# Attention with a shared expert: q and k split once and stacked through DRAM, output normalised transposed, one large burst every second step

## The chip, the cores and the metric

The kernel runs on one core of a Trainium2 chip. The metric is the device time of one execution in microseconds (us); lower is better.

## The reference

Eight batches of 512 rows with 256 columns are normalised row by row (`xn`). The output is `x + attention(xn) + ffn(xn)`:

```python
def holo_linear(x, basis, phase, amp):            # rank 32
    resonance = jnp.einsum('bli,hi->blh', x, basis)
    return jnp.einsum('blh,oh->blo', resonance, amp * jnp.cos(phase))
q, k, v = (split_heads(holo_linear(x, ...)) for each of q, k, v)   # 16 heads of 16
attn = softmax(jnp.einsum('bhqd,bhkd->bhqk', q, k) * 16 ** -0.5)
out = holo_linear(merge_heads(jnp.einsum('bhqk,bhkd->bhqd', attn, v)), basis_o, phase_o, amp_o)

# ffn: 8 experts of width 352, the best 2 of each row, plus a shared expert of width 704
y = einsum('te,etd->td', combine, expert_out)
return y + (silu(x @ sw_gate) * (x @ sw_up)) @ sw_down
```

All is float32. A matrix product is made exact enough by splitting each operand into a high part (rounded to the format float32r, which TensorE multiplies fast) and a low part (what the rounding left), and adding three products: high by high, low by high, high by low.

## The kernel before

There are three stages. An early one normalises the rows, transposes and splits them (`xn_T_split` in DRAM) and finds the experts of each row. A second one runs 72 tiles of gathered rows through the experts and stores them (`expert_rows`). The late stage, from about 423 us to the end, is the one that the change rebuilds. It does attention and the shared expert for the 8 batches.

The late stage is a software pipeline written out by hand. Each engine runs the same loop `slots`: for each batch b four slots g = 0 to 3, one for each group of four heads, with three slots ahead and two behind; and in each slot eight steps t (`STEPS`). In a step TensorE (PE) does, in this order of its queue:

- `score_T`: the transposed scores of two heads of group g into the pair of banks `st_pair` (two matmuls, 512 columns each). ScalarE (ACT) makes the exponentials of them (`exponent`, `prob`). There is one such pair of banks, so `score_T` of a step waits for `exponent` of the step before.
- `score`: the scores of two heads of the next group into `s_pair`, three steps ahead (`AHEAD`). VectorE (DVE) takes their row maxima (`maximum`, `top`). There is one such pair too, so `score` waits for the `maximum` before it.
- at t = 5 `turn_max`: the maxima, split by `split_max` at t = 4, are transposed; ACT copies them (`max_rows`), and SyncE (SP) puts them by DMA into two extra rows of `q_rows`, so that `score_T` subtracts the maximum. `score_T` of the next slot's t = 0 waits for this.
- at even t `values`: the product of `prob` with the values and a column of ones, which gives the sum of the exponentials with it, into `ot_bank`.
- the rest: small products and the "bursts" of the shared expert.

The rest stands thus in the kernel before. In every slot, at t = 0 to 3, `project` makes q and k of the group after next, for two pairs of heads each, in `m_bank`. The weight `wq_rows` holds each head's columns three times, so that the product comes out as three stacked copies; ACT copies it rounded (`qk_high`) and DVE forms, with a factor of 0 or -1 for each partition (`q_minus`, `k_minus`), the high or low part for each copy (`qk_split`). Four projections in each slot are one chain: each waits for the `qk_split` before, since `m_bank` is one bank. The three ranks-32 products (`low_rank`, n = q, k, v) stand at g = 1, t = 4 and 6, and g = 2, t = 4. The shared expert (`gate_up_shared`: six matmuls of 512 columns) has six tiles f of its width, each a gate and an up; they stand at g = 1 and 3 in every step t = 1 to 6. The sixth tile has only 64 of 128 rows. `tanh` (ACT), `gate_shared`, `hidden_shared` (DVE), `hidden_high` (ACT) and `hidden_low` (GpSimd, POOL) follow. `down_shared` (18 matmuls of 256 columns) stands at g = 2, odd t. The output of batch b-1 is done in g = 0 of batch b: for each 128 rows `turn_o` transposes `o_T`, DVE takes the reciprocal of the 16 sums of each row and multiplies (`normalise`), `turn_back` transposes again, ACT and DVE split; then `low_rank_o` (t = 6) and `project_o` (t = 7) into two banks, which `add_o` adds.

All four compute queues are in order. A wait in one holds all that stands behind it. DMAs are issued by SP, in order too, but for the gathers of `expert_rows`, which POOL issues.

## Time and profile before

| | |
|---|---|
| median of 3 runs | 1241.31 us (1239.57 to 1248.31) |
| the profiled execution | 1241.18 us, of which its span is 1239.4 us |
| busy: PE, DVE, ACT, POOL | 1055.1, 767.2, 601.5, 339.2 us |
| mean granted clock of TensorE | 0.899 of full speed |
| DMA | 73.43 MB, mean 59 GB/s |

The span is the stretch from the first to the last instruction that the profile holds; the 1.8 us around it stay as they are in all sums. "Granted clock" is the share of full speed that TensorE was given. A line of a group gives its busy time, the mean of one instruction in ns and the idle time of its engine before it. Matmuls overlap, so what one costs its queue is read from the starts of two that follow one another, not from its duration.

### The profile page before, as it was taken

How to read it: one execution, taken by the hardware profiler on the slowest of the kernel's cores; microseconds unless marked ns; L12 is line 12 of the kernel's file. 1: busy time of each engine (PE TensorE's matmuls, PEld its weight loads, DVE VectorE, ACT ScalarE, POOL GpSimd, SP SyncE). 2: the span in 40 equal slices, each digit the busy share in tenths (PEclk: the TensorE clock that was granted, in tenths of full speed). 3: DMA queues.
4: the chain of work that ended last, by engine and by line, in shares of the span. 5: the costliest groups of instructions: out<-in, count | busy, mean ns of one | idle time of the engine just before them, and what ended most of it. 6: DMA issues, size and time to landing. Idle time of an engine off the chain costs nothing.

```text
span 1239.4 us, 18708 instructions
## 1 busy us (share of the span) xinstructions
PE 1055.1 (85%) x6090; PEld 698.1 (56%) x6091; DVE 767.2 (62%) x1264; ACT 601.5 (49%) x945; POOL 339.2 (27%) x292
## 2 busy tenths in 40 slices
PE   1750699999999768998998998998998999999986
PEld 1740699999999633554454454454454454454442
DVE  6679533443443356677767767767767767767732
ACT  0231244444444425555655655555555656556652
POOL 1045332222222216106205205304303313312410
PEclk8555599999999967898998998999999999999995
DMA  7664052222222002002102102102102101100100
GB/s 218 237 240 140 17 173 73 68 68 74 69 68 74 33 1 87 1 1 69 35 2 69 36 2 69 36 2 69 36 2 69 35 2 61 44 2 18 53 2 17
DMA packets 47888, 73.43 MB, mean 59 GB/s; under 512 B 7304, under 2 KB 40656, under 8 KB 45776
## 3 DMA queue, kind: packets, MB, share of 16 engines
q1 hardware_dynamic: 41296, 54.74, 12.9%
q0 software_dynamic: 6528, 17.83, 5.1%
q8 instruction: 40, 0.66, 0.2%
q14 instruction: 24, 0.20, 0.1%
HBM read 45.82 MB, written 26.21 MB: 58 GB/s over the span
## 4 chain that ended last, share of the span: by engine, by line
PE 67%; DVE 15%; issue 8%; ACT 5%; DMA 2%; POOL 1%; another core or an unknown queue 1%; SPq 1%; DVEq 0%; ACTq 0%
PE bank L939 10%; PE bank L961 8%; PE st_pair L950 6%; PE bank L841 6%; PE bank L1002 6%; PE s_pair L823 5%; PE st_pair L823 5%; PE s_pair L903 4%; PE bank L892 4%; PE bank L976 3%; ACT prob L682 2%; DVE q_rows L1343 2%; PE bank L831 2%; ACT qk_hi L647 2%; DVE top L1351 2%
## 5 line engine op out<-in xcount | busy, mean ns | idle before, releaser
L1351 DVE TENSOR_REDUCE top<-s_pair 128x2 f32<-128x1024 f32 x256 | 313.3, 1224 | 163.7 <-PE s_pair L903 159.8
L682 ACT ACTIVATE prob<-st_pair 128x1024 f32<-128x1024 f32 x256 | 261.5, 1022 | 217.8 <-PE st_pair L950 214.1
L534 POOL TENSOR_TENSOR h_T<-h_f,h_T 128x512 fp32r<-128x512 f32 (+1 forms) x48 | 61.7, 1286 | 495.9 <-ACT h_T L665 495.9
L950 PE MATMUL st_pair<-q_rows,k_rows 50*128 50x512 f32 x512 | 144.0, 509 | 29.3 <-ACT prob L682 28.6
L950 PEld LDWEIGHTS st_pair<-q_rows,k_rows 50*128 50x128 f32 x512 | 55.8, 189 | 179.9 <-issue 117.6
L939 PE MATMUL bank<-xT_b,w_sh 128*128 128x512 f32 (+1 forms) x576 | 153.8, 402 | 0.0
L961 PE MATMUL bank<-prob,v_ones 128*32 128x512 f32 x1024 | 149.3, 658 | 1.1 <-ACT prob L682 1.1
L903 PE MATMUL s_pair<-k_rows,q_rows 48*128 48x512 f32 x512 | 122.2, 433 | 9.8 <-DVE top L1351 5.5
L510 POOL DMA_INDIRECT xg<-xn_rows,token_of x72 | 68.5, 951 | 210.8 <-PE bank L806 178.5
L939 PEld LDWEIGHTS bank<-xT_b,w_sh 128*128 128x128 f32 (+1 forms) x576 | 101.4, 181 | 32.1 <-issue 6.3
L841 PE MATMUL bank<-w_exp,c_hT 128*128 (+1 forms) x648 | 95.4, 292 | 1.0 <-ACT c_y L617 1.0
L823 PE MATMUL s_pair<-w_exp,xg_T 128*128 x432 | 78.2, 331 | 10.6 <-issue 8.9
L647 ACT ACTIVATE qk_hi<-bank 128x512 fp32r<-128x512 f32 x128 | 76.0, 594 | 22.3 <-PE bank L892 20.8
L1002 PE MATMUL bank<-w_sh,h_T 128*128 128x256 f32 (+1 forms) x576 | 83.4, 294 | 0.0
L841 PEld LDWEIGHTS bank<-w_exp,c_hT 128*128 128x128 f32 (+1 forms) x648 | 82.1, 191 | 1.4 <-issue 1.4
L1002 PEld LDWEIGHTS bank<-w_sh,h_T 128*128 128x128 f32 (+1 forms) x576 | 75.5, 194 | 8.6 <-issue 3.6
L823 PE MATMUL st_pair<-w_exp,xg_T 128*128 x432 | 77.2, 328 | 1.0 <-DVE xg_T L1308 1.0
L823 PEld LDWEIGHTS s_pair<-w_exp,xg_T 128*128 128x128 f32 x432 | 70.6, 192 | 12.9 <-issue 12.8
L1299 DVE TENSOR_TENSOR c_h<-c_sil,s_pair 128x352 f32<-128x352 f32 x36 | 18.8, 521 | 86.2 <-PE s_pair L823 86.2
L823 PEld LDWEIGHTS st_pair<-w_exp,xg_T 128*128 128x128 f32 x432 | 70.7, 192 | 1.4 <-issue 1.4
L903 PEld LDWEIGHTS s_pair<-k_rows,q_rows 48*128 48x128 f32 x512 | 56.1, 194 | 25.5 <-DVE top L1351 15.6
L544 POOL DMA_INDIRECT y_b<-expert_rows,slot_of x64 | 61.3, 958 | 18.3 <-issue 17.7
(195 smaller groups left out, 1472.4 us busy)
## 6 DMA issues: line engine op xcount, KB each, us to landing
expert_rows<-c_y SPq DMA_DIRECT2D x72, 128.0 KB, 1.7
xn_T_split<-x_T SPq DMA_DIRECT2D x8, 1024.0 KB, 4.6
xT_b<-xn_T_split SPq DMA_DIRECT2D x8, 1024.0 KB
x_all<-in_L_attn_x_dram SPq DMA_DIRECT2D x8, 512.0 KB, 5.6
xn_rows<-x_n SPq DMA_DIRECT2D x8, 512.0 KB, 4.9
o_b<-in_L_attn_x_dram SPq DMA_DIRECT2D x8, 512.0 KB, 3.8
out_dram<-o_b SPq DMA_DIRECT2D x16, 256.0 KB, 2.3
raw_all<-in_L_ffn_w_gate_dram SPq DMA_DIRECT2D x8, 352.0 KB, 4.3
```

The costliest lines, as they stand in the source:

```text
L510: pool.indirect_dma_start(xg[s % 4][:, :], None, xn_dram, bass.IndirectOffsetOnAxis(token_of[:, s:s + 1], 0)).then_inc(c_x[s % 4], 16)
L534: pool.tensor_tensor(h_T[0:m, LO, f, :], h_f[f % 2][0:m, :], h_T[0:m, HI, f, :].bitcast(F32), ALU.subtract).then_inc(p_h, 1)
L647: act.activation(qk_hi[n % 2][:, :], m_bank[:, :], ACT.Copy).then_inc(a_qk, 1)
L682: act.activation(prob[kt % 2][:, 2 * jp:2 * jp + 2, :].rearrange("p j l -> p (j l)"), st_pair[:, :], ACT.Exp, scale=HD ** -0.5).then_inc(a ...
L823: ins = pe.matmul(gu_bank[i % 2][n][:, 0:F], xg_T[i % 2][:, a * KT + k, :], w, start=(m == 0 and k == 0), stop=(m == 2 and k == KT - 1))
L841: ins = pe.matmul(y_bank[:, 0:D], c_hT[i % 2][0:n, a, k, :], w, start=(m == 0 and k == 0), stop=(m == 2 and k == FT - 1))
L903: ins = pe.matmul(s_pair[:, i * 512:(i + 1) * 512], q_rows[g][r:r + 48, jp, qt * P:(qt + 1) * P], k_rows[g][r:r + 48, jp, :], start=True, ...
L939: ins = pe.matmul((g_bank, u_bank)[n][0:m, :], w_sh[:, a, o:o + m], xT_bs[b % 2][:, c, k, :], start=(i == 0), stop=(i == 5))
L950: ins = pe.matmul(st_pair[:, i * 512:(i + 1) * 512], k_rows[g][r:r + QKV_ROWS, jp, kt * P:(kt + 1) * P], q_rows[g][r:r + QKV_ROWS, jp, :], ...
L961: ins = pe.matmul(ot_bank[32 * j:32 * j + 32, :], v_ones[:, kt, 4 * g + j, :], prob[kt % 2][:, j, :], start=(kt == 0), stop=(kt == TPB - 1))
L1002: ins = pe.matmul((g_bank, u_bank)[t % 2][:, 0:D], h_T[0:m, a, f, t * P:(t + 1) * P], w_sh[0:m, c, S_GU + f * D:S_GU + (f + 1) * D], start ...
L1351: dve.tensor_reduce(top[g % 2][:, :, jp, qt], s_pair[:, :].rearrange("p (i k) -> p i k", i=2), AX_X, ALU.max).then_inc(d_max, 1)
```

## The change

- The rank-32 products of q, k and v are one product (`low_rank`: 96 rows, at g = 0, t = 2). ACT copies them rounded, DVE forms the low part, and SP stores them to DRAM (high part twice, low part once) and loads them back stacked (`r_all`).
- q and k are projected whole, two halves each: four projections in a batch instead of sixteen (`project`, g = 1, even t). ACT and DVE split each once (`qk_hi`, `qk_lo`). SP stores the parts to DRAM (12 stores in a batch) and loads the stacked rows for each group (16 loads). `wq_rows`, `wk_rows`, `q_minus` and `k_minus` go. The maxima take 2 DMAs in a slot, not 4.
- The output of each group goes to DRAM (`store_o`), and for two groups SP loads the values and the sums, spread over all 128 partitions (`load_o`: `ao` and `o_sum`, each 128 by 512). DVE takes the reciprocal of `o_sum` and multiplies, at t = 5 of g = 2 and g = 0. ACT and POOL split. The transposes `turn_o` and `turn_back` go.
- `project_o` adds onto the bank of `down_shared`, and `add_o` goes.
- The sixth tile's gate and up are one burst (`g_bank`, 64 rows each): 11 bursts in place of 12. Bursts stand at odd t alone, in g = 2, 3 and the next batch's 0; `down_shared` in g = 1 of the next batch; `low_rank_o` at g = 0, t = 7.
- In the last batch `down_shared` runs before `low_rank_o`. One more slot stands ahead of the first batch.

```diff
+        def unit(b, g, t):
+            if t % 2 == 0:
+                return None, None, None
+            n = t // 2
+            c, what, i = ((b - 1, "gate" if n in (0, 2) else "up" if n == 1 else "out", 4 + n // 2),
+                          (b - 1, "down", n),
+                          (b, ("gate", "up")[n % 2], n // 2),
+                          (b, ("gate", "up")[n % 2], 2 + n // 2))[g]
+            return (what, c, i) if there(c) else (None, None, None)
...
+            def store_low_rank(b):
+                wait(sp, r_in, b * 16)
+                parts = r_dram.rearrange("n (c h) l -> n c h l", c=3)
+                wait(sp, a_r, b + 1)
+                for c in range(2):
+                    sp.dma_start(parts[:, c, :, :], r_hi[:, :].bitcast(F32)).then_inc(r_st, 16)
+                wait(sp, d_r, b + 1)
+                sp.dma_start(parts[:, 2, :, :], r_lo[:, :].bitcast(F32)).then_inc(r_st, 16)
...
+            def store_qk(b, n):
...
+                for c in ((0, 1), (0, 2))[which]:
+                    sp.dma_start(dst[:, c, :, :], qk_hi[half][:, :].bitcast(F32)).then_inc(qk_st[half], 16)
+                wait(sp, d_qk, b * 4 + n + 1)
+                sp.dma_start(dst[:, (2, 1)[which], :, :], qk_lo[half][:, :].bitcast(F32)).then_inc(qk_st[half], 16)
...
+            def load_o(b, p):
+                for i in range(2):
+                    wait(sp, ot_st[i], (2 * b + p + 1) * 16)
+                wait(sp, p_ao, 2 * b + p)
...
+                sp.dma_start(ao[:, :], v[:, 0, :, :]).then_inc(ao_in, 16)
+                sp.dma_start(o_sum[:, :], v[:, 1, :, :]).then_inc(ao_in, 16)
...
             def slot(b, g):
+                if there(qb):
+                    load_rows(qb, qg)
+                if g == 2 and there(b - 1):
+                    store_out(b - 1, 1)
+                if g == 2 and there(b):
+                    load_x_b(b)
+                if there(pb):
+                    store_o(pb, pg)
+                    if pg % 2:
+                        load_o(pb, pg // 2)
                 if g == 0 and there(b + 1):
-                    load_xT(b + 1)
+                    store_low_rank(b + 1)
+                if g == 1 and there(b + 1):
+                    for n in range(2):
+                        store_qk(b + 1, n)
...
+                if there(nb):
+                    load_max(nb, ng)
...
+            def ao_low(b, p):
+                wait(pool, a_ao, 2 * b + p + 1)
+                pool.tensor_tensor(ao_T[:, LO, p, :], ao[:, :], ao_T[:, HI, p, :].bitcast(F32), ALU.subtract).then_inc(p_ao, 1)
...
+                hidden_low(b, 0)
+                ao_low(b, 0)
+                for f in range(1, 5):
+                    hidden_low(b, f)
+                ao_low(b, 1)
                 hidden_low(b, 5)
...
+            def ao_high(b, p):
+                wait(act, d_ao, 2 * b + p + 1)
+                wait(act, b_res, b)
+                act.activation(ao_T[:, HI, p, :], ao[:, :], ACT.Copy).then_inc(a_ao, 1)
...
+                    if t == 5 and pg % 2 and there(pb):
+                        ao_high(pb, pg // 2)
+                    what, c, i = unit_before(b, g, t)
+                    if what == "up" or what == "gate" and i == SFT - 1:
+                        hidden_high(c, i)
+                    what, c, i = unit(b, g, t)
+                    if what == "gate":
+                        tanh(c, i)
...
+            def project_o(b, t):
+                wait(pe, d_res, b + 1)
+                pe.matmul(down_bank(b, t)[:, 0:D], ro[:, t * P:(t + 1) * P], w_rows[:, 3, :], start=False, stop=True).then_inc(b_dn, 1)
...
+            def normalise(b, p):
+                wait(dve, ao_in, (2 * b + p + 1) * 32)
+                dve.reciprocal(o_sum[:, :], o_sum[:, :]).then_inc(d_inv, 1)
+                wait(dve, d_inv, 2 * b + p + 1)
+                dve.tensor_tensor(ao[:, :], ao[:, :], o_sum[:, :], ALU.mult).then_inc(d_ao, 1)
...
+                    if g == 0 and t == 2 and there(b + 1):
+                        low_rank_low(b + 1)
+                    if g == 1 and t % 2 == 0 and there(b + 1):
+                        qk_low(b + 1, t // 2)
+                    if t == 5 and pg % 2 and there(pb):
+                        normalise(pb, pg // 2)
```

## Rows read from the trace of the kernel before

**Rows 1.** The page, part 5: costliest groups, busy time, mean ns, idle time before.
```profile
L1351 DVE TENSOR_REDUCE top<-s_pair 128x2 f32<-128x1024 f32 x256 | 313.3, 1224 | 163.7 <-PE s_pair L903 159.8
L682 ACT ACTIVATE prob<-st_pair 128x1024 f32<-128x1024 f32 x256 | 261.5, 1022 | 217.8 <-PE st_pair L950 214.1
L534 POOL TENSOR_TENSOR h_T<-h_f,h_T 128x512 fp32r<-128x512 f32 (+1 forms) x48 | 61.7, 1286 | 495.9 <-ACT h_T L665 495.9
...
L647 ACT ACTIVATE qk_hi<-bank 128x512 fp32r<-128x512 f32 x128 | 76.0, 594 | 22.3 <-PE bank L892 20.8
```

**Rows 2.** Busy time by stretch: batch 1, last batch, the end.
```profile
core 0: us, PE busy (x) PEld busy (x) DVE busy (x) ACT busy (x) POOL busy (x), PEclk, DMA share, GB/s
564.00:659.30 95.30, 88.09 (x492) 46.68 (x493) 68.64 (x91) 55.39 (x78) 27.40 (x24) 0.96 0.11 34
1136.00:1217.80 81.80, 70.58 (x404) 33.96 (x403) 45.26 (x62) 47.28 (x61) 24.73 (x22) 0.92 0.09 27
1217.80:1239.40 21.60, 12.42 (x42) 7.04 (x42) 6.41 (x15) 2.73 (x6) 0.00 (x0) 0.50 0.07 25
```

**Rows 3.** TensorE's timeline in slot g = 1: start us, duration, engine, line, operation.
```profile
594.20 0.50 PE L950 MATMUL st_pair<-q_rows,k_rows 50*128 50x512 f32 x2
...
594.85 0.50 PE L892 MATMUL bank<-r_k,wk_rows 97*128 97x512 f32 x1
595.19 1.55 PE L939 MATMUL bank<-xT_b,w_sh 128*128 128x512 f32 x6
596.67 1.06 PE L961 MATMUL bank<-prob,v_ones 128*32 128x512 f32 x8
597.66 0.50 PE L950 MATMUL st_pair<-q_rows,k_rows 50*128 50x512 f32 x2
```

**Rows 4.** The same timeline: transposed maxima, and down with the next product.
```profile
605.63 0.60 PE L918 MATMUL bank<-ident_f,top_parts 128*8 128x128 f32 x4
...
623.64 2.26 PE L1002 MATMUL bank<-w_sh,h_T 128*128 128x256 f32 x16
...
626.54 1.62 PE L976 MATMUL bank<-xT_b,basis_T 128*96 128x512 f32 x6
```

**Rows 5.** TensorE's timeline where the maxima alone, then the exponentials alone, set the pace.
```profile
445.62 0.50 PE L903 MATMUL s_pair<-k_rows,q_rows 48*128 48x512 f32 x2 [2.14 <-DVE top L1351]
447.44 0.80 PE L903 MATMUL s_pair<-k_rows,q_rows 48*128 48x512 f32 x2 [0.69 <-DVE top L1351]
...
1203.87 0.50 PE L950 MATMUL st_pair<-q_rows,k_rows 50*128 50x512 f32 x2 [0.19 <-ACT prob L682]
1205.49 0.50 PE L950 MATMUL st_pair<-q_rows,k_rows 50*128 50x512 f32 x2 [1.12 <-ACT prob L682]
```

**Rows 6.** VectorE's groups of the whole run, by shape: a product and the reciprocals.
```profile
L1366 DVE SCALAR_TENSOR_TENSOR h_f<-h_f,bank 128x512 f32<-128x512 f32 x40 | 27.1, 678 | 0.0
L1389 DVE RECIPROCAL o_inv<-bank 128x16 f32<-128x16 f32 x32 | 8.1, 252 | 23.1 <-PE bank L1018 21.2 <-remote 1.5
...
L1211 DVE RECIPROCAL row<-row 128x32 f32<-128x32 f32 x1 | 0.4, 353 | 0.0
```

**Rows 7.** Busy time by stretch in slot g = 0 of batch 1 (columns of rows 2).
```profile
571.00:574.50 3.50, 3.43 (x24) 1.51 (x22) 2.39 (x6) 1.41 (x2) 2.74 (x3) 1.00 0.38 112
574.50:578.00 3.50, 1.86 (x7) 1.36 (x8) 2.30 (x4) 0.91 (x2) 1.89 (x2) 0.75 0.37 101
578.00:582.00 4.00, 4.00 (x18) 1.46 (x17) 2.94 (x7) 1.89 (x5) 3.23 (x4) 0.50 0.03 10
```

**Rows 8.** The page, part 6: DMA issues, KB each, median us from issue to landing.
```profile
xn_T_split<-x_T SPq DMA_DIRECT2D x8, 1024.0 KB, 4.6
...
out_dram<-o_b SPq DMA_DIRECT2D x16, 256.0 KB, 2.3
```

**Rows 9.** TensorE's timeline ahead of the first batch: two projections, first score, first transposed score.
```profile
433.29 0.80 PE L892 MATMUL bank<-r_q,wq_rows 96*128 96x512 f32 x1 [1.47 <-DVE q_rows L1343]
435.56 0.79 PE L892 MATMUL bank<-r_k,wk_rows 97*128 97x512 f32 x1 [1.47 <-DVE q_rows L1343]
...
442.89 0.60 PE L903 MATMUL s_pair<-k_rows,q_rows 48*128 48x512 f32 x2
...
469.02 0.49 PE L950 MATMUL st_pair<-q_rows,k_rows 50*128 50x512 f32 x2 [0.30 <-DMA q_rows<-top_T]
```

501 lines of the change are left out of this document (225 added, 276 removed).

## The prediction, written before the changed kernel ran

> **What bounds the kernel now.** The profile is read in four passes. First the stretches: in the middle of the late stage a batch takes 95.3 us, TensorE is busy for 88.1 of them and VectorE for 68.6; the last batch takes 81.8 us, since nothing follows it, and an end of 21.6 us stands behind it [rows 2]. So the late stage goes by TensorE's queue, and VectorE is next. Second, what an item costs TensorE's queue, from the starts in its timeline: the two score products of a step 0.65 us (594.20 to 594.85), a projection 0.34, a burst 1.48, the values 0.99 [rows 3]; down with the score products behind it 2.90, so down alone 2.25; the four transposes of the maxima last 0.60 and are taken at 0.4 [rows 4]. Third, the loops through the single banks: where only maxima are due a step takes 1.82 us (445.62 to 447.44), where only exponentials are due 1.62 [rows 5], though the maximum itself takes 1.22 and the exponential 1.02 [rows 1]; 0.6 us is product and hand-over. Fourth, the clock: in slot g = 0, where TensorE waits for the transposes' other engines, it was busy for 1.86 of 3.5 us, and stood at 1.2 GHz (granted 0.50) for the next 4 us, against 1.00 before it [rows 7].
>
> What stays of a batch's items for TensorE in the kernel before, added up: 32 pairs of scores 20.8, 16 values 15.8, 12 bursts 17.8, 4 downs 9.0, 16 projections 5.4, 3 rank products of 1.5 each 4.5, and maxima, value projections, turns, `low_rank_o` and `project_o` about 8.5: 82 us. The other 13 us are waits and half clock.
>
> **What goes from TensorE.** 12 projections (4.1), 2 rank products (3.0), one burst (1.5), and the turns (8 groups of transposes, at the 0.4 of rows 4 about 3): 11.6 us, leaving 70. With the projections goes their chain through `m_bank` in the four slots (2.27 us for each link where it stands bare [rows 9]). VectorE loses 16 splits of 0.7 and gets 4.
>
> **The steps after.** In g = 2, 3 and 0 four steps hold a gate and an up. TensorE's own work is 4 x 0.65 + 2 x 0.99 + 2 x 1.48 = 7.5 us. But ACT's queue now matters. From the start of the even step behind an up burst: score lands and its maximum ends at 2.1; the hidden product (0.68 [rows 6]) at 2.8; its copy on ACT (0.59 [rows 1]) at 3.4; the exponential behind this copy at 4.5, and the next transposed score waits for that. TensorE's items in these two steps last 3.77. So 0.75 is lost, and the four steps take 8.3. A slot has two such fours, 0.4 for the transposed maxima, and 0.6 for `split_max` on VectorE and the copy of the maxima on ACT, which push the same chain: 17.6 for g = 3. g = 2 has a value projection more, 0.6: 18.2. g = 0 has that and the rank product: 19.7. g = 1 holds 4 downs with `project_o` (2.4 each) and 4 projections: 5.2 + 4.0 + 1.4 + 9.5 + 0.4 = 20.4, and the other engines have room there. Sum: 75.9 us.
>
> **The reciprocal.** This is the item that the diff hides. Before, VectorE took reciprocals of 16 sums for each row, 252 ns each [rows 6]. Now it takes 512 for each partition: `values` writes each head's sum into 16 rows, and all of them are loaded and inverted. No row shows that size. From 16 to 32 elements it rises from 252 to 353 ns: at 6.3 ns for each more, 512 would take 3.4 us; at the 11 ns for each that 353/32 gives, 5.6. A product of 512 elements takes only 0.68 [rows 6], so it isn't an ordinary operation. I take 4.3, between the ends, because part of both short rows is fixed and the source of one is PSUM. The Trainium skill ("VectorE: DVE Perf Modes", First, the fixed hardware budget) says that the reciprocal is an iterative division repeated 8 times; at its 0.96 GHz an estimate is 4.3 us and a little for the start. No row here shows it directly.
>
> With the multiplication `normalise` holds VectorE for 5.0 us, at t = 5. Behind it stands the next `maximum`. `ao_high` waits for it in ACT's queue, and behind that stand `tanh` and the exponential of t = 6, for which the transposed score of t = 7 waits. From the start of t = 5: maximum done 2.2, normalise 7.2, copy 7.8, tanh 8.4, exponential 9.5; without it t = 7 begins at 5.3. So 4.2 us stall in g = 2 and 4.2 in g = 0. The work moved before it doesn't cover it: the bank pairs are single, so TensorE can't run ahead. POOL's part (1.29 [rows 1]) is done before `low_rank_o` asks for it at about 22 us of g = 0.
>
> An idle stretch of over 4 us is longer than the one that brought the clock down in rows 7. There the low clock covered at least 5.8 us (1.75 in the second stretch, 4 in the third), which is 2.9 us lost if it is all work. The price lies between 0 and 2.9 for each stall; I take 2.0, because part of the low clock falls into the idle time. Batch: 75.9 + 2 x 4.2 + 2 x 2.0 = 88.3 us, 7.0 less than now.
>
> **DMAs, costed at nothing in the loop.** A batch gets 3 + 12 + 4 stores and 1 + 16 + 4 loads. Landing takes 2.3 us for 256 KB and 4.6 for 1 MB [rows 8]; SP has about 50 issues in 88 us. The tight place is g = 2. SP waits there for the last q, k store, issues four loads, waits until the output store has landed (`o_st`, in `load_x_b`), then stores o, waits for it and loads it. With 2.3 us for each landing and 0.6 for an issue the sums are there 12.2 us into the slot; VectorE asks for them at 13.4. The cover is 1.2 us. Four landings lie in series in it. In g = 0 the rank-32 stores and their load have until the next slot, some 15 us.
>
> **The start.** One rank product with its split goes (3), four legs through DRAM come (store and load of the rank rows, of q and k), each between 2.3 and 4.6, taken at 3.0, with 3 us of issues that nothing covers: the first score moves from 442.9 [rows 9] by +12 to 455. From there to the first transposed score were 26.1 us; without bursts it is 8 maxima of about 2 and 5.5 for the transposes and the DMA: 21.5. Preparation loses about 1.5 us of copies. First batch: 475 in place of 469.0. By the Trainium skill ("DMA: Bandwidth & Descriptors", Why a DMA increments its semaphore by 16 and not by 1) a copy is spread over a number of engines that divides the slowest dimension of both sides. The rank stores have 3 there and the q, k stores 8. By that and the megabyte row these legs would take about 10 us longer at the start, and the time would be 1211; no row shows a store of this form.
>
> **First and last batch, and the end.** Batch 0 has no bursts in g = 0 and 1, so the loop of the maxima sets 16.5 each; with g = 2 (18.2 + 6.2) and g = 3 it takes 75, against 95 now. The last batch: g = 0 24.4 (no rank product), g = 1 19.0, g = 2 23.6, g = 3 15: 82, as now. The end now has gate and up of the last tiles and all the downs: values and copy 2.6, store and load of o 5.8, `normalise` 5.0; then, behind it in the queues of ACT and VectorE, the last tile: copy 0.6, tanh 0.6, two products 1.4, copy 0.6, POOL 1.3; that is 17.9. `down_shared` waits for it: 9.0, and 2 for the low clock; `low_rank_o` and its split 3.5; adds 1.5; the store 3. Together 37 against 21.6.
>
> **Sum.** 1241.2 (the profiled run) + 6 (start) - 20 (batch 0) - 6 x 7.0 + 0 + 15.4 = 1200.6. It stands 0.1 us from the median. Forecast: **1201 us**.
>
> **The rivals.**
>
> - *Forecast*, 0.47: stalls of 4 to 5 us and a clock that falls. Its own range is 1180 to 1229.
> - *A short stall*, 0.22: the reciprocal takes 3.4 and the clock holds, as it does in g = 1 to 3 now. Each stall costs 3.3 in place of 6.2; 15 of them in the loop and 3 us at the end: 1201 - 46 = 1155, and up to 1180.
> - *Nothing to measure*, 0.18: the change takes work from TensorE but VectorE gives it back. At 5.6 for the reciprocal and 2.9 for the clock a batch takes 75.9 + 11.0 + 5.8 = 92.7: with the first and last batches and the end about 35 more, 1236. For it: VectorE is busy for 72% of a batch already.
> - *The sums come late*, 0.13, the other side: with the traffic of q, k and o beside it, each of the four landings in g = 2 takes 4.6 us, as a megabyte does now. Then `ao_in` comes at 21.4, VectorE and ACT stand 8 us longer in every batch, and the time is 1201 + 64 = 1265. It decides from a landing of 3.9 us on: 1.6 more for each of four, less the cover of 1.2, is 5.1 us for each of 8 batches, all of the gain. Against it: the DMA share is 0.11 now [rows 2].
>
> About 1% is what a measurement of this kernel can tell from no change. Faster by over 1% are the first two, 0.69; within 1% the third, 0.18; slower the last, 0.13. The range reaches from the middle of the second into the third: 1160 to 1242.
>
> **What would show it.** Reciprocal 128x512 at 4.3 us, 16 of them, and as many waits of `maximum` and the exponential behind it. Batches of 88 us, with g = 3 the shortest at 17.6. The granted clock at 0.5 after each `normalise`. The first transposed score at 475. VectorE's wait for `ao_in` near zero in the loop. Wrong would be: a reciprocal at the rate of a product (then 1140 or so); a wait for `qk_in` or `m_in` at the head of slots; g = 3 at 20 us or more, which would say that the chain through the bursts and copies is longer than its 0.75.

## The result: the changed kernel is slower

| | before | after |
|---|---|---|
| median of 4 runs each, same chip | 1242.38 us | 1358.91 us (1354.63 to 1361.31) |
| ratio after / before | | 1.0952, 95% interval 1.0904 to 1.0999 |
| span of the profiled run | 1239.4 us | 1359.6 us |
| first transposed score | 469.0 [rows 9] | 498.3 |
| a batch in the middle (of 6) | 95.3 [rows 2] | 104.5 |
| the last batch, the end | 81.8, 21.6 [rows 2] | 96.5, 41.6 |

I had forecast 1201, in a range of 1160 to 1242. Against my sum the profiled run has 23 us more at the start (498.3 for 475), 21.5 in batch 0 (96.5 for 75), 6 x 16.2 in the middle batches (104.5 for 88.3), 14.5 in the last batch (96.5 for 82) and 4.6 at the end: 161 us, which is all of the miss (1361.3 against 1200.6). By slots, the 97 us of the six middle batches are 58 in g = 2 and 51 in g = 1, less 11 in g = 0 and 1 in g = 3.

The costliest groups of the page after (line, engine, operation, xcount, then busy us and mean ns, then idle time before them and what ended it). They answer to [rows 1] and [rows 6]:

```profile
L1395 DVE TENSOR_REDUCE top<-s_pair 128x2 f32<-128x1024 f32 x256 | 313.5, 1225 | 271.8 <-PE s_pair L1002 248.0
L783 ACT ACTIVATE prob<-st_pair 128x1024 f32<-128x1024 f32 x256 | 261.4, 1021 | 229.5 <-PE st_pair L1046 203.4
L1046 PE MATMUL st_pair<-q_rows,k_rows 50*128 50x512 f32 x512 | 139.8, 542 | 153.0 <-ACT prob L783 146.3
...
L1433 DVE RECIPROCAL o_sum<-o_sum 128x512 f32<-128x512 f32 x16 | 53.6, 3349 | 79.6 <-DMA o_sum<-o_rows 79.6
```

Maximum and exponential are what they were. The reciprocal takes 3.35 us, and VectorE stands 79.6 us ahead of it for a DMA. The four slots of batch 4 (start and end, length, then busy us of PE, PEld, DVE, ACT, POOL, granted clock, DMA share, GB/s), g = 0, 1, 2, 3:

```profile
913.90:938.19 24.29, 20.31 (x103) 9.66 (x103) 17.77 (x18) 13.15 (x18) 6.14 (x5) 0.88 0.32 92
938.19:966.85 28.66, 24.91 (x149) 15.29 (x148) 14.30 (x18) 11.93 (x15) 16.26 (x16) 0.92 0.64 182
966.85:1000.82 33.97, 18.88 (x97) 9.13 (x96) 16.32 (x16) 11.66 (x15) 4.83 (x3) 0.75 0.51 141
1000.82:1017.95 17.13, 16.71 (x93) 7.78 (x92) 12.45 (x14) 10.93 (x14) 2.57 (x2) 1.00 0.12 35
```

I had given 25.9, 20.4, 24.4 and 17.6. So g = 3, which has few transfers (a DMA share of 0.12) and no normalise, is as forecast; g = 2 is 10 us too long and g = 1 8 us. Inside g = 2 SyncE's own timeline (start, length, line, what is issued) tells why:

```profile
964.76 0.80 SPq L495 DMA_DIRECT2D qk_rows<-qk_lo  x1
965.61 1.20 SPq L461 DMA_DIRECT2D xT_b<-xn_T_split  x1
971.82 0.80 SPq L506 DMA_DIRECT2D k_rows<-qk_rows  x2
972.66 0.90 SPq L506 DMA_DIRECT2D q_rows<-qk_rows  x2
973.61 0.43 SPq L469 DMA_DIRECT2D out_dram<-o_b  x1
978.72 0.40 SPq L465 DMA_DIRECT2D o_b<-in_L_attn_x_dram  x1
979.21 0.45 SPq L518 DMA_DIRECT2D o_rows<-o_T  x1
983.93 0.65 SPq L525 DMA_DIRECT2D ao<-o_rows  x1
984.63 0.62 SPq L526 DMA_DIRECT2D o_sum<-o_rows  x1
```

and what VectorE, ACT and TensorE do meanwhile (in brackets the idle time before it and what ended it):

```profile
990.62 3.35 DVE L1433 RECIPROCAL o_sum<-o_sum 128x512 f32<-128x512 f32 x1 [10.77 <-DMA o_sum<-o_rows]
...
994.73 0.63 ACT L794 ACTIVATE ao_T<-ao 128x512 fp32r<-128x512 f32 x1 [14.22 <-DVE ao L1435]
...
996.82 0.80 PE L1046 MATMUL st_pair<-q_rows,k_rows 50*128 50x512 f32 x2 [14.64 <-ACT prob L783]
997.41 0.63 PE L1002 MATMUL s_pair<-k_rows,q_rows 48*128 48x512 f32 x2
997.97 2.93 PE L1035 MATMUL bank<-xT_b,w_sh 128*128 128x512 f32 x6
```

The slot begins at 966.85. Four landings lie one behind another in SP's queue: q, k's last store to the load of its rows (964.8 to 971.8, 7.1 us), the output's store to x's load (5.1), o's store to its load (4.7), and o_sum's load to the reciprocal (6.0). The sums are there 23.8 us into the slot; I had 12.2 in the forecast and 21.4 in the rival "The sums come late". VectorE asks for them at 13.0 (I said 13.4). After the 14.6 us of TensorE's wait, a transposed score lasts 0.80 and a burst 2.93, where they lasted 0.50 and 1.65 before it; the clock granted from 996.8 to 1000.8 is 0.50, which is 1.2 GHz.

### The profile page after: what moved, and what is told of

It reads as the page before. It is cut to its first block, busy times and chain, and to the rows that moved or that the text cites. A ratio compares the mean times of both kernels' runs of the same rounds, so it can differ in the third digit from the quotient of the medians.

```text
span 1359.6 us, 17757 instructions
## 1 busy us (share of the span) xinstructions
PE 1002.1 (74%) x5658; PEld 661.9 (49%) x5659; DVE 710.6 (52%) x1070; ACT 539.6 (40%) x817; POOL 357.0 (26%) x306
## 4 chain that ended last, share of the span: by engine, by line
PE 40%; DMA 26%; DVE 14%; issue 8%; ACT 6%; SPq 5%; another core or an unknown queue 2%; POOL 0%; DVEq 0%; POOLq 0%; ACTq 0%
DMA low_rank_rows<-r_lo 6%; PE bank L943 6%; PE s_pair L925 5%; PE st_pair L925 5%; DMA qk_rows<-qk_lo 5%; PE bank L1035 4%; DMA o_rows<-o_T 4%; PE st_pair L1046 4%; PE bank L1094 4%; DMA o_sum<-o_rows 4%; ACT prob L783 4%; DMA r_all<-low_rank_rows 3%; PE s_pair L1002 2%; DMA out_dram<-o_b 2%; DVE top L1395 2%
## 5 line engine op out<-in xcount | busy, mean ns | idle before, releaser
L1046 PE MATMUL st_pair<-q_rows,k_rows 50*128 50x512 f32 x512 | 139.8, 542 | 153.0 <-ACT prob L783 146.3
L1046 PEld LDWEIGHTS st_pair<-q_rows,k_rows 50*128 50x128 f32 x512 | 51.7, 199 | 319.2 <-ACT prob L783 261.2
L1035 PE MATMUL bank<-xT_b,w_sh 128*128 128x512 f32 x528 | 156.3, 435 | 0.0
L1057 PE MATMUL bank<-prob,v_ones 128*32 128x512 f32 x1024 | 145.7, 643 | 0.0
L1035 PEld LDWEIGHTS bank<-xT_b,w_sh 128*128 128x128 f32 x528 | 99.4, 202 | 38.5 <-issue 18.4
L1433 DVE RECIPROCAL o_sum<-o_sum 128x512 f32<-128x512 f32 x16 | 53.6, 3349 | 79.6 <-DMA o_sum<-o_rows 79.6
L652 POOL TENSOR_TENSOR o_b<-o_b,y_b 128x1024 f32<-128x1024 f32 x8 | 18.8, 2347 | 259.5 <-DMA o_b<-in_L_attn_x_dram 259.5
L1002 PEld LDWEIGHTS s_pair<-k_rows,q_rows 48*128 48x128 f32 x512 | 55.1, 210 | 54.5 <-DVE top L1395 24.2
L1094 PEld LDWEIGHTS bank<-w_sh,h_T 128*128 128x128 f32 (+1 forms) x504 | 71.7, 212 | 13.2 <-issue 7.0
L647 POOL TENSOR_SCALAR y_b<-y_b,share 128x256 f32<-128x256 f32 x64 | 58.0, 918 | 31.1 <-DMA y_b<-expert_rows,slot_of 31.1
```

The source lines that it names most:

```text
L647: pool.tensor_scalar(y_b[:, t, k, :], y_b[:, t, k, :], share[:, b * TPB + t, k:k + 1], None, ALU.mult).then_inc(p_ys, 1)
L1002: ins = pe.matmul(s_pair[:, i * 512:(i + 1) * 512], q_rows[g][r:r + 48, jp, qt * P:(qt + 1) * P], k_rows[g][r:r + 48, jp, :], start=True, ...
L1035: ins = pe.matmul((g_bank, u_bank)[n][:, :], w_sh[:, a, o:o + P], xT_bs[b % 3][:, c, k, :], start=(i == 0), stop=(i == 5))
L1046: ins = pe.matmul(st_pair[:, i * 512:(i + 1) * 512], k_rows[g][r:r + QK_ROWS, jp, kt * P:(kt + 1) * P], q_rows[g][r:r + QK_ROWS, jp, :], s ...
L1057: ins = pe.matmul(ot_bank[32 * j:32 * j + 32, :], v_ones[:, kt, 4 * g + j, :], prob[kt % 2][:, j, :], start=(kt == 0), stop=(kt == TPB - 1))
L1094: pe.matmul(down_bank(b, t)[:, 0:D], h_T[0:m, a, f, t * P:(t + 1) * P], w_sh[0:m, c, S_GU + f * D:S_GU + (f + 1) * D], start=(i == 0), sto ...
```

## Experiments

Chips differ: the kernel before took 1218 to 1246 us on those used. So each run is given as a ratio to the kernel before on its own chip, and slots are compared by length. The changed kernel, e11, e13, e14, e16 and e17 were timed four times or more and have an interval; every other ratio rests on one time of the edited kernel. A slot's length is from its first transposed score to the next slot's, a mean over batches 1 to 6; "start" is the first transposed score of all.

| kernel | ratio | start | batch 0 | g0 | g1 | g2 | g3 | batch |
|---|---|---|---|---|---|---|---|---|
| changed | 1.095 | 498.3 | 96.5 | 24.1 | 28.9 | 34.0 | 17.5 | 104.5 |
| e1_late0 | 1.084 | 498.9 | 95.1 | 24.5 | 30.3 | 23.8 | 24.4 | 102.9 |
| e2_norecip | 1.072 | 497.0 | 93.1 | 21.9 | 31.8 | 30.9 | 17.3 | 101.9 |
| e3_rank16 | 1.095 | 493.5 | 92.4 | 24.1 | 30.6 | 33.4 | 17.3 | 105.4 |
| e4_order | 1.047 | 493.4 | 95.1 | 23.8 | 28.0 | 26.4 | 17.5 | 95.8 |
| e5_queue | 1.086 | 493.2 | 98.8 | 24.3 | 26.2 | 17.3 | 32.8 | 100.6 |
| e6_pieces | 1.063 | 494.3 | 92.8 | 24.1 | 27.2 | 17.5 | 28.0 | 96.7 |
| e8_order_only | 1.051 | 497.7 | 93.0 | 24.2 | 25.8 | 27.5 | 17.6 | 95.0 |
| e9_wide_only | 1.044 | 484.7 | 87.1 | 23.9 | 23.9 | 29.7 | 17.5 | 95.1 |
| e15_wide_order | 1.006 | 481.6 | 84.1 | 24.0 | 23.7 | 24.1 | 17.4 | 89.2 |
| e7_wide | 1.002 | 481.0 | 88.0 | 24.2 | 23.9 | 22.9 | 17.6 | 88.6 |
| e10_late_pieces | 0.999 | 482.3 | 79.0 | 24.2 | 25.1 | 17.9 | 22.0 | 89.2 |
| e11_end | 0.996 | 479.5 | 85.2 | 24.3 | 24.1 | 22.9 | 17.6 | 88.9 |
| e12_wide_norecip | 0.951 | 480.2 | 78.9 | 21.0 | 24.3 | 18.2 | 17.1 | 80.6 |
| e13_compact | 0.959 | 481.2 | 69.7 | 19.8 | 32.6 | 17.3 | 17.1 | 86.8 |
| e14_tuned | 0.952 | 481.7 | 69.2 | 18.3 | 29.3 | 17.3 | 17.1 | 82.1 |
| e16_swap | 0.948 | 480.8 | 77.4 | 18.3 | 32.1 | 17.3 | 17.1 | 84.9 |
| e17_start | 0.925 | 474.3 | 69.9 | 18.3 | 25.8 | 17.3 | 17.1 | 78.6 |

e2_norecip and e12_wide_norecip leave the division by the sums out. They price a part, and are no versions to use.

One thing disturbs g = 1 in some of these runs and not in others. In it ACT and VectorE at times stand idle together for 4 to 7 us, the last 2 to 5 of them after the product that they wait for is done, and nothing in the trace releases them (the last section has an example). I call this a pause. In all ACT stands so for 20.9 us in the changed kernel, 24.4 in e1, 5.3 in e2, 42.6 in e3, 9.0 in e4 and 33.5 in e16. In the other runs ACT never stands for 1 us behind such a product. So g = 1 of these six can't be compared with g = 1 of the others without this.

The theory at the outset was that the sums come late, because of the legs through DRAM and because SP's queue is in order. The rival was that the reciprocal's block, and the clock behind it, are the price.

### The first four: one edit each on the changed kernel

**e1_late0**

```diff
...
-                    if t == 5 and pg % 2 and there(pb):
-                        normalise(pb, pg // 2)
+                    if t == 5 and g == 3 and now:
+                        normalise(b, 0)
+                    if t == 5 and g == 0 and there(b - 1):
+                        normalise(b - 1, 1)
```

> The changed kernel with one edit: pair 0 of each batch is normalised in step 5 of g=3, not of g=2, a slot after its sums were asked for. Against the changed kernel's 1359 us. Late sums (the wait for the two stores and the load of the sums is what lengthens g=2, and not the reciprocal): g=2 falls from 32 to 35 us to about 24, g=3 grows from 17.5 to about 23 (reciprocal 3.3 us and clock 2), so about 5 us less in each of 8 batches: 1320. The reciprocal and the clock that falls behind it are the bulk: what g=2 loses g=3 gains, each by 5 to 6 us, and the time stays within 10 us of 1359. If transfers run late everywhere, g=2 stays over 30 us with the wait gone elsewhere.

ACT's and POOL's parts of the normalise move with it. 1343.49 us against 1239.58: 15 us less than the changed kernel, where late sums had been given 39 and the reciprocal under 10. g = 2 fell by 10 us, as the theory of late sums has it, and g = 3 rose by 7 (5.5 expected). g = 2 didn't get to 18, since another wait appeared at its end, in TensorE's timeline:

```profile
885.06 0.80 PE L1049 MATMUL st_pair<-q_rows,k_rows 50*128 50x512 f32 x2 [5.55 <-DMA q_rows<-top_T]
```

The maxima's rows for g = 3 stand in SP's queue behind the load of o, so they are as late as the sums. Everything behind the four landings is late, not the sums alone.

**e2_norecip**

```diff
-                dve.reciprocal(o_sum[:, :], o_sum[:, :]).then_inc(d_inv, 1)
+                dve.tensor_copy(o_sum[:, :], o_sum[:, :]).then_inc(d_inv, 1)
```

> The changed kernel with the reciprocal of the sums left out (a copy of the same tile stands in its place, so the attention output is multiplied by its sum and not divided). The copy should take 0.7 us where the reciprocal takes 3.35. Reciprocal as the main cost: 16 stalls shrink by 2.65 us each and by the clock behind them (2 us): 75 us less, 1285. Late sums as the main cost: only the 2.65 us each, 42 us less, and g=2 still 29 to 32 us long: about 1317. If the sums come so late that the stall is set elsewhere, under 25 us less.

1329.31 us, 1.072: 30 us less than the changed kernel by the medians, nearer to the 42 of late sums than to the 75 of the reciprocal, and g = 2 still takes 30.9. But the 30 us are not the whole price of the block. g = 0 and g = 2 are shorter by 2.2 and 3.1, and g = 1 is longer by 2.9: there TensorE asks for the rank rows sooner and waits longer for them. Its waits for them in g = 1 of batches 1 to 6 (total, times, longest), in the changed kernel and here:

```profile
PE bank L992 <- DMA r_all<-low_rank_rows: 9.4, 6, 2.2
```

```profile
PE bank L992 <- DMA r_all<-low_rank_rows: 24.0, 6, 4.7
```

While the transfers are late, much of what a shorter reciprocal gives back is lost at the next of them; e12 prices the block where they are not.

**e3_rank16**

```diff
-    r_dram = nc.dram_tensor("low_rank_rows", (3, 96, L), F32).ap()
+    r_dram = nc.dram_tensor("low_rank_rows", (96, 3, L), F32).ap()
...
-                    sp.dma_start(parts[:, c, :, :], r_hi[:, :].bitcast(F32)).then_inc(r_st, 16)
+                    sp.dma_start(r_dram[:, c, :], r_hi[:, :].bitcast(F32)).then_inc(r_st, 16)
...
-                sp.dma_start(r_all[:, :, :].bitcast(F32), r_dram.rearrange("n r l -> r n l")).then_inc(r_in, 16)
+                for c in range(3):
+                    sp.dma_start(r_all[32 * c:32 * c + 32, :, :].bitcast(F32),
+                                 r_dram[:, c, :].rearrange("(n h) l -> h n l", n=3)).then_inc(r_in, 16)
```

> The changed kernel with the three low-rank projections in another order in their scratch rows (row by row, so that a store is 96 pieces and not 3) and loaded back in three parts. Theory that a copy is slow because its first dimension is short (3 or 8): a 192 KB store lands in about 2.5 us in place of 5.9, the hand-off before the first score shrinks by about 8 us and the waits for it in the batches (36 us in all) by about 20: 1330. Theory that such a copy is slow because of its size and its place behind other copies: under 5 us less, 1355 to 1359.

1356.74 us. SP issues the store of the low part and then, when it has landed, the load; first the changed kernel, then this one:

```profile
433.68 0.67 SPq L479 DMA_DIRECT2D low_rank_rows<-r_lo  x1
440.24 0.36 SPq L484 DMA_DIRECT2D r_all<-low_rank_rows  x1
```

```profile
434.84 0.30 SPq L478 DMA_DIRECT2D low_rank_rows<-r_lo  x1
436.90 1.30 SPq L484 DMA_DIRECT2D r_all<-low_rank_rows  x3
```

6.6 us from issue to issue became 2.1, with the same bytes. The mechanism is there, and the start came 4.8 us earlier. The expected 1330 was missed, but the run doesn't show that the batches gained nothing. TensorE's wait for these rows in g = 1 (9.4 us in the changed kernel, see e2) is gone from the trace, and the pauses named above add up to twice as much: seven of them, one in each g = 1 from batch 1 on, against four.

```profile
ACT prob L784 <- remote: 42.6, 7, 6.9
```

In batch 0, which has no such pause, g = 1 is 23.9 us for 24.9. What the rank rows' layout alone is worth in the other batches stays open.

**e4_order**

```diff
-                if g == 2 and there(b - 1):
-                    store_out(b - 1, 1)
-                if g == 2 and there(b):
-                    load_x_b(b)
                 if there(pb):
                     store_o(pb, pg)
                     if pg % 2:
                         load_o(pb, pg // 2)
+                if g == 2 and there(b - 1):
+                    store_out(b - 1, 1)
+                if g == 2 and there(b):
+                    load_x_b(b)
...
-                if g == 1 and there(b + 2):
+                if g == 3 and there(b + 2):
                     load_xT(b + 2)
```

> The changed kernel with the queue's order alone changed: the 1 MB load of xT is asked for in g=3, not g=1, and in g=2 the stores and loads of the attention output stand ahead of the output's store and x's load. Theory that the sums of pair 0 come late because other copies stand ahead of them (5.1 us in which the queue waits behind x's load, and a store and a load that share the engines with 1.5 MB): the sums are asked for 5 to 8 us earlier, g=2 is 5 to 8 us shorter in each of 8 batches, 1300 to 1320. Theory that the legs themselves are slow (4.4 us of a load, the stores of 128 rows) and the queue's order matters little: 1345 to 1359.

1297.44 us, 1.047: better than the expected range. g = 2 went from 34.0 to 26.4. So the order makes up about half of the whole loss.

### Transfers in the right order, and stores that land sooner

**e5_queue** puts e1's and e4's edits together and loads the maxima ahead of o in g = 2.

> The kernel with the queue's order changed (e4_order, 1297) and pair 0 normalised in step 5 of g=3 as in e1_late0, and in g=2 the maxima's rows are loaded ahead of the load of the attention output. In e1_late0 TensorE stood 5 to 6 us at the head of g=3 for these maxima (q_rows<-top_T), since their load stands in SP's queue behind that of the attention output. Theory that the queue's order is all that holds the sums: no wait for sums and none for maxima is left in g=2 and g=3; g=2 falls from 26.3 to about 20 and g=3 rises from 17.6 to 23: 8 x (-6 + 5.5), 1290 to 1297. Rival that g=2 is long by something else than transfers (its own work is 23 us, as in e1_late0): g=2 stays at 23 or more and the time rises to 1310 or above.

1327.80 us, 1.086, a clear miss. g = 2 was 17.3, but g = 3 32.8. I had put x's load behind the maxima and o, and this is what followed (SP, POOL, ACT, TensorE):

```profile
864.05 0.39 SPq L465 DMA_DIRECT2D o_b<-in_L_attn_x_dram  x1
...
868.23 2.34 POOL L654 TENSOR_TENSOR o_b<-o_b,y_b 128x1024 f32<-128x1024 f32 x1 [25.84 <-DMA o_b<-in_L_attn_x_dram]
...
871.88 0.60 ACT L762 ACTIVATE h_f<-bank 128x512 f32<-128x512 f32 x1 [7.24 <-POOL h_T L631]
...
873.44 0.80 PE L1051 MATMUL st_pair<-q_rows,k_rows 50*128 50x512 f32 x2 [7.51 <-ACT prob L786]
```

POOL's addition of x stands in its queue ahead of the hidden tiles' low halves, tanh waits for their buffer, and the exponential stands behind tanh. A wait had been moved from one queue into three others.

**e6_pieces** has on top of it, for pair 0:

```diff
+            def invert(b, i):
+                if i == 0:
+                    wait(dve, ao_in, (2 * b + 1) * 32)
+                for k in (((0, 1), (2, 3), (4,), (5, 6), (7,))[i]):
+                    dve.reciprocal(o_sum[:, 64 * k:64 * k + 64], o_sum[:, 64 * k:64 * k + 64]).then_inc(d_inv, 1)
...
+                    if t < 5 and g == 3 and now:
+                        invert(b, t)
```

> As e5_queue, but the reciprocal of pair 0 in 8 pieces of 64 columns, spread over steps 0 to 4 of g=3. Theory that what a normalise costs is one block of 3.35 us ahead of a maximum, and the clock that falls behind it: g=3 falls by 4 to 5.5 us against e5_queue, 8 times: 32 to 44 us less. Theory that VectorE's total work is what counts: nothing changes, or it is slower by 8 x 0.5 us for the pieces' fixed part.

1300.08 us, 1.063: 27.7 less than e5 on the same chip (32 to 44 expected), g = 3 from 32.8 to 28.0 (a piece of 64 columns takes 524 ns, so 6.3 ns for each column beyond: (3344 - 524) / 448). Here the pieces filled time in which VectorE stood waiting anyway; e10 shows that it is not a general gain.

**e8_order_only** is e4_order with xT's load left in g = 1.

> As e4_order (1297), but the 1 MB load of xT stays where the change put it, in g=1 ahead of the loads of rows; only the order within g=2 is changed. Theory that waiting in SP's queue is the price (5.1 us behind the output's store in every g=2): most of the 62 us is kept, 1305 to 1315. Theory that the bytes of xT compete with the stores and loads behind them: about half is lost again, 1325 to 1340.

1285.39 us against 1222.82, 1.051, where e4_order has 1.047: most of the gain comes from the order within g = 2, and xT's place is worth little.

**e7_wide** is e4_order with e3's layout, and the same for q and k:

```diff
-                dst = qk_dram[b % 2, which, 8 * half:8 * half + 8].rearrange("h (c r) l -> h c r l", c=3)
+                dst = qk_dram[b % 2, which, 8 * half:8 * half + 8].rearrange("h (r c) l -> (h r) c l", c=3)
...
-                    sp.dma_start(dst[:, c, :, :], qk_hi[half][:, :].bitcast(F32)).then_inc(qk_st[half], 16)
+                    sp.dma_start(dst[:, c, :], qk_hi[half][:, :].bitcast(F32)).then_inc(qk_st[half], 16)
```

> As e4_order (1297), with the scratch rows of the low-rank projections and of q and k laid out so that every store is one row for each partition (a first dimension of 96 or 128 in place of 3 and 8), with the same bytes. In e3_rank16 the low part of the rank rows landed 2.1 us after its issue where it took 5.9. Theory that a short first dimension makes these copies slow: the first transposed score comes 12 us earlier than in e4_order (493.4), g=1 and g=2 lose the waits for r_all (11 us in all) and for qk_rows (40 us of SP's queue): 1265 to 1280. Theory that only the queue's order matters by now: 3 to 6 us at the start and nothing else, about 1292.

1225.61 us against 1222.82, 1.002. By the ratio to e4 that is 22 us beyond the best that was expected; and a batch of 88.6 us, where the forecast had 88.3. SP's waits for the last store of q and k from the first transposed scores on, in the changed kernel and here (total, times, longest):

```profile
SPq L62 <- DMA qk_rows<-qk_lo: 35.9, 7, 6.2
```

```profile
SPq L62 <- DMA qk_rows<-qk_lo: 14.6, 7, 2.1
```

and its g = 2, batch 4, where the reciprocal starts with no wait for its sums:

```profile
886.49 0.34 SPq L519 DMA_DIRECT2D o_rows<-o_T  x1
889.04 0.66 SPq L526 DMA_DIRECT2D ao<-o_rows  x1
889.75 0.62 SPq L527 DMA_DIRECT2D o_sum<-o_rows  x1
...
895.34 3.34 DVE L1434 RECIPROCAL o_sum<-o_sum 128x512 f32<-128x512 f32 x1
```

**e9_wide_only** is the layout alone, with SP's old order.

> The changed kernel with only the layout of the scratch rows of the rank projections and of q and k altered (every store one row for each partition); SP's queue in its old order. e7_wide had both and came to 1.002 of the kernel before, e4_order with the order alone to 1.047, the changed kernel stands at 1.095. If the two causes add, this alone gives 1.095 - 0.045 = 1.05. If the wait for a store of q and k in front of everything in g=2 is what makes the sums late, more than that, 1.02 to 1.04, and g=2 falls from 34 to 26 or less. If the order is needed for it to count, less: 1.07 to 1.09.

1272.36 us, 1.044. So the four corners are 1.095, 1.047 (order), 1.044 (layout), 1.002 (both): the two causes add, at some 0.05 each. The first two corners have the pauses in g = 1; e8, this run and e15 below have none, and by them the layout is worth 0.045 (1.051 to 1.006) and the order within g = 2 0.038 (1.044 to 1.006). These three ran on three chips; their batches of 95.0, 95.1 and 89.2 us say the same, 5.8 and 5.9 us a batch. Each cause is thus worth 0.04 to 0.05, 50 to 60 us.

g = 2 is shorter by 4.3 with the layout alone, and the order shortens it by 7 to 8. g = 1 is 5 shorter than in the changed kernel, but only 2 to 3 of these are the layout: with the old layout and no pauses g = 1 takes 25.8 to 27.2 (e8, e5, e6), with the new one 23.7 to 24.1 (e15, e7, e9, e11).

Of the four landings in g = 2 the layout shortens one, that of the last q, k store, from 7.1 to 2.9:

```profile
903.25 0.46 SPq L496 DMA_DIRECT2D qk_rows<-qk_lo  x1
...
906.16 0.79 SPq L507 DMA_DIRECT2D k_rows<-qk_rows  x2
```

The output's store takes 5.0 to 5.7 us here and in e4, e7, e8 and e15 as well, and the sums' load 5.2 to 6.0 wherever VectorE waits for it (medians of batches 1 to 6). The new order doesn't shorten these two. It takes the output's store, and x's load behind it, out of the sums' way. o's store takes 4.3 to 5.3 but for e7, where it takes 2.6.

**e15_wide_order**, e7_wide with xT's load in g = 1, was to part the two edits of e4_order once more, with the stores wide.

> As e7_wide (wide stores, new order in g=2) with xT's load left in g=1, where the change put it: it parts the two edits of e4_order. g=2 was 30 us with wide stores alone and 22.9 with both. Theory that the wait of SP's queue behind x's load is what is left: g=2 at 23 to 24. Theory that the 1 MB just ahead of the stores competes with them: g=2 at 26 or more.

1225.61 us against 1217.85, 1.006, and g = 2 at 24.1. The queue's order is the main part; with the 1 MB ahead of the rows' loads g = 2 is 1.2 us longer than in e7, and the batch 0.6.

### What is left: the reciprocal

**e12_wide_norecip** is e7_wide with e2's edit.

> As e7_wide, with the reciprocal replaced by a copy of the same tile (0.7 us for 3.35), so that the attention output is multiplied by its sum and not divided. It prices the reciprocal where its sums are no longer late. My prediction's model: the block goes through VectorE, ACT and the transposed scores one for one, and the clock behind it is priced at up to 2.9 us; so g=0 and g=2 fall by 2.65 and up to 2 more each: 21.5 to 19.6 and 20.2 to 18.3, the whole time by 43 to 75 us. If something else ends the wait in g=2 (x, the maxima), g=2 stays over 21.

1159.40 us, 0.951. g = 2 (batch 4) in e7_wide and here:

```profile
882.65:905.54 22.89, 18.92 (x97) 9.17 (x96) 16.14 (x16) 11.66 (x15) 4.82 (x3) 0.89 0.52 139
```

```profile
848.39:866.56 18.17, 17.16 (x98) 8.19 (x97) 13.20 (x16) 11.66 (x15) 1.53 (x1) 1.00 0.58 157
```

The copy took 0.43 us, so the block is 2.9 us shorter; the slot is 4.7 us shorter (g = 0: 3.2), and the granted clock is 1.00 in place of 0.89. 18.2 is what the forecast had for g = 2 without its stall.

**e10_late_pieces** is e7_wide with pair 0's reciprocal in pieces in g = 3, the maxima ahead of o, and x left where it was.

> As e7_wide (batches of 88.6 us: g=0 24.2, g=1 23.9, g=2 22.9, g=3 17.6), with pair 0 normalised in g=3 in 8 pieces of the reciprocal, the maxima's load ahead of that of the attention output, and x's load left ahead of both, since in e5_queue it stood behind the maxima and POOL, and ACT behind it, waited up to 12 us in g=3. Theory that a block of 3.35 us ahead of a maximum is the price of a normalise: g=2 falls to about 18, g=3 rises to 19 or 20, 2.5 to 3.5 us less a batch, 20 to 28 in all. Rival that the chain ao to ao_T to exponential costs the same wherever it stands: g=2 and g=3 together stay at 40 to 41.

1218.17 us, 0.999. g = 2 and g = 3 together take 39.9 us for 40.5: the rival holds. Cut up, the reciprocal still lies in a chain of maximum, score and exponential that has no slack to put it in. It must become smaller.

**e11_end** is e7_wide with the last batch's last hidden tile ahead of its normalise (VectorE's edit; ACT and POOL have the same):

```diff
...
-                    if t == 5 and pg % 2 and there(pb):
+                    if t == (7 if b == NB else 5) and pg % 2 and there(pb):
                         normalise(pb, pg // 2)
```

> As e7_wide, but behind the last batch the last hidden tile (gate, up, its halves) comes ahead of the normalisation of pair 1 on VectorE, ACT and POOL. In e7_wide TensorE stood 12.8 us before the last downs, for h_T. Theory that the normalisation in front of that tile is the price of the end: h_T is there 8 to 9 us earlier, the downs (13.5 us of TensorE) cover the normalisation, and the time falls by 8 to 9 us: 0.995 of the kernel before. Rival that the downs then run at half clock for longer: 3 to 5 us only, 0.998.

0.9963 (0.9936 to 0.9990). From the start of the last g = 3 to the end it took 44.1 us where e7_wide took 55.1, 11 us less: the downs now cover the normalise. TensorE's wait ahead of them fell from 12.8 to 4.2 us, and the first 36 of their products took 6.6 us where they took 8.9. The saving shows in the stretch; the ratio moved by 0.006, where 11 us would be 0.009.

**e13_compact** takes the reciprocal of 128x32. One row of sums a head is loaded as 16 short rows, inverted, stored, and loaded back into 16 rows a head. It has e7's layout and xT's place, and further moves that the compact tile needs: pair 0 is multiplied in g = 3 and pair 1 in g = 1, low_rank_o stands in g = 1, and the last hidden tile comes ahead of the multiplication. The transfers:

```diff
+                sp.dma_start(o_few[:, :], o_dram[2 * p:2 * p + 2].rearrange("g (j u c) (s m) -> (g j) u c s m", j=4, u=2, s=16)[:, 1, 0, :, :]).then_inc(ao_in, 16)
...
+                sp.dma_start(inv_dram.rearrange("h (s m) -> (h s) m", s=16), o_few[:, :]).then_inc(inv_st, 16)
...
+                sp.dma_start(o_sum[:, :], inv_dram.rearrange("h (r l) -> h r l", r=1).to_broadcast([8, 16, L])).then_inc(inv_in, 16)
```

> The changed kernel with wide stores and xT's load in g=3, and with the reciprocal taken of 128x32 in place of 128x512: one row of sums a head is loaded as 16 short rows, inverted (0.35 us by the row of 128x32), stored, and loaded back into 16 rows a head; pair 0 is multiplied in g=3 and pair 1 in g=1, so that the two added transfers have half a slot or more; low_rank_o stands in g=1 behind the first down, and the last hidden tile ahead of the multiplication. Theory that a block of 3.35 us on VectorE is 66 us of the whole (e12_wide_norecip stood at 0.951 of the kernel before, with the end as it was): 0.945 to 0.96. Rival that the added transfers and waits in SP's queue cost as much as the block did (maxima or x late, as in e5_queue): 0.98 to 1.02, with a wait for q_rows<-top_T or o_sum in the trace.

0.9586 (0.9541 to 0.9630), as expected (0.945 to 0.96). g = 0, 2 and 3 are 19.8, 17.3 and 17.1: a whole slot is near TensorE's own work. But g = 1 is 32.6, since low_rank_o stands there now, and project_o waits for its split:

```profile
755.80 0.40 PE L1025 MATMUL s_pair<-k_rows,q_rows 48*128 48x512 f32 x2
759.24 0.39 PE L1122 MATMUL bank<-w_rows,ro 96*128 96x256 f32 x1 [3.04 <-issue]
759.47 3.45 PE L1117 MATMUL bank<-w_sh,h_T 128*128 128x256 f32 x18
```

**e14_tuned** moves low_rank_o ahead of the first down and the small operations around it.

> As e13_compact (0.959 of the kernel before; slots of 19.8, 31 to 34, 17.3, 17.1 us), with four moves around the head of g=1, where TensorE stood 2.4 us before step 0 and 3.4 us before step 3 and had 1.2 GHz for about 16 us behind them. low_rank_o goes ahead of the first down (step 1), project_o of tile 0 into step 2, the product and the copies of pair 1 ahead of the q, k copies of step 0, and the last hidden tile's second product and copy behind the maximum and the exponential of step 7. Theory that a wait at the head of g=1 costs its own length and the half clock behind it: g=1 falls to 23 or 24, and 8 slots give back 55 to 70 us: 0.905 to 0.92. Rival that the clock stays low in g=1 for the bursts of down themselves: g=1 stays at 28 or more, 0.93 to 0.95.

0.9516 (0.9461 to 0.9570), short of 0.905 to 0.92: g = 1 fell only to 29.3, as TensorE now stood 2.3 us for POOL's half of ao_T.

**e16_swap** puts low_rank_o behind the first down.

> As e14_tuned (0.952 of the kernel before, g=1 29 us), with low_rank_o behind the first down in step 1, not ahead of it. In e14_tuned TensorE stood 2.3 us there for the low half of ao_T, and low_rank_o and the first down behind it ran at half clock for about 1.2 us more than their length. Theory that the wait is covered by the down (2.6 us) and the clock holds: g=1 at 25.5, 7 times 3.5 us less: 0.93. Rival that the wait comes back one step later, for project_o behind the two halves of ro: g=1 at 27 or more, 0.94 to 0.95.

0.9484 (0.9440 to 0.9528), on a chip where g = 1 took 32.1. Its trace has six of the pauses there, 33.5 us in all for ACT, so the run doesn't decide. In e17 below, on a chip without them, the same g = 1 takes 25.8, as expected of this run.

**e17_start** moves nine fills of constants:

```diff
...
-            for g in range(NG):
-                for h in range(2):
-                    ins = dve.memset(k_rows[g][64 * h + 32:64 * h + 64, :, :].bitcast(F32), -1.0)
...
                     if g == 0 and t == 2 and there(b + 1):
                         low_rank_low(b + 1)
+                        if b == -1:
+                            constants()
```

> As e16_swap (0.948 of the kernel before; first transposed score at 480.8), with the nine fills of constants on VectorE (k_rows and v_ones, 0.91 us each, eight of them new in the change) behind the split of the first rank projection in place of ahead of it. In the changed kernel this split came at 433.0, 10.8 us after TensorE had ended the projection at 422.3, and everything at the start hangs behind it. Theory that these fills are 10 us of the start: r_lo at 423.5 to 424, the first transposed score at 471 to 473, 0.940 to 0.942. Rival that the fills then stand before the q, k splits and delay those instead: 476 to 480, no change to measure.

0.9251 (0.9211 to 0.9290), 1127.82 us against 1218.87. This version beats both kernels. It is better than the 0.940 to 0.942 expected, since e16's 0.948, from which that was worked out, had the pauses in it. In the changed kernel VectorE filled k_rows from 422.82 on, and only then split the rank projection, which TensorE had ended at 422.3:

```profile
422.82 0.91 DVE L1381 MEMSET k_rows<- 32x1024 f32 x1 [5.24 <-DMA expert_rows<-c_y]
...
432.19 0.91 DVE L1383 MEMSET v_ones<- 128x1024 f32 x1 [0.28 <-issue]
433.02 0.62 DVE L1423 TENSOR_TENSOR r_lo<-bank,r_hi 96x512 fp32r<-96x512 f32 x1
...
446.05 0.79 PE L992 MATMUL bank<-r_all,w_rows 96*128 96x512 f32 x1 [23.78 <-DMA r_all<-low_rank_rows]
```

With the fills behind the split it comes at 422.28, and the first q, k projection at 430.06. The first transposed score came 6.5 us earlier than in e16, 8 to 10 expected: the fills delay the first q, k split (434.1 for the second projection, 3.3 us of wait), so both expectations have a part. The four slots of batch 4, g = 0, 1, 2, 3:

```profile
779.51:797.81 18.30, 17.07 (x97) 8.06 (x97) 13.19 (x16) 11.99 (x16) 2.58 (x2) 1.00 0.71 181
797.81:823.55 25.74, 24.64 (x154) 14.91 (x154) 15.82 (x21) 12.75 (x17) 18.31 (x19) 1.00 0.69 226
823.55:840.90 17.35, 17.15 (x98) 8.28 (x98) 12.44 (x15) 11.01 (x14) 3.38 (x2) 1.00 0.47 127
840.90:858.02 17.12, 16.50 (x95) 7.78 (x94) 13.05 (x15) 11.44 (x15) 5.57 (x5) 1.00 0.38 90
```

TensorE is busy for 75.4 of 78.5 us, at full clock in all four. In the changed kernel it was 80.8 of 104.1.

## Why the prediction was wrong

**The step that failed: "DMAs, costed at nothing in the loop".** It rested on a landing of 2.3 us, from [rows 8], for every transfer, and a cover of 1.2 us for four of them in series. I named the chain and the point from which it decides (3.9 us a landing), and gave it 0.13. The landings were 7.1, 5.1, 4.7 and 6.0, so the sums were there at 23.8 and not at 12.2, and VectorE stood 10.8 us for them. The row of 2.3 is of one store to a tensor with 128 rows, in batches with a DMA share of 0.11 [rows 2]; here the share was 0.51, at 141 GB/s, and the same store took 5.1. Of the three stores among the four, only that of q and k has the short first dimension. Traffic as a mean of the slot doesn't settle the others: in e7 g = 2 moved 139 GB/s, and o's store took 2.6 there for 4.7. What stands just ahead of it in the queue differs (x's 512 KB in the changed kernel, k's and q's loads in e4, where it took 4.6, and in e7 the same loads 2 us earlier), but no run parts this from the layout. What should have been done with that step: such a price bounds the cost from below only, and a chain of four with 1.2 us of cover in front of two engines' queues is the likeliest place to fail.

Two causes of it are shown, and they add: the order in SP's queue and the form of the stores, each worth 0.04 to 0.05. With both mended the changed kernel's batch is 88.6, against 88.3 in the forecast. That they agree is luck: the slots are 24.2, 23.9, 22.9 and 17.6 for 25.9, 20.4, 24.4 and 17.6, so g = 0 and g = 2, taken 3.2 us too long, hide a g = 1 taken 3.5 too short. And the time is the kernel before's (e7_wide, 1.002; the forecast is 0.967). Its span of 1223.9 is 25 us over the forecast's 1198.8: 6 at the start, 13 in batch 0, 2 in the middle batches, 4 behind them. The rest of the distance is that the kernel before took 1222.8 us on that chip and not 1241. Of the form only this is shown: with the first dimension at 96 or 128 in place of 3 and 8, the same bytes land in 2 to 3 us and not in 6 to 7. The Trainium skill ("DMA: Bandwidth & Descriptors", Why a DMA increments its semaphore by 16 and not by 1) has the mechanism, fewer engines for a short slowest dimension. e3 and e9 agree with it, though no row names the engines that a copy used. I had priced this rule at 10 us at the start and left it out of every batch, where it cost most. The loads of o and of its sums have a first dimension of 8 too, on the side of DRAM, in every run from the changed kernel to e12; none alters it, so whether the sums' 5.2 to 6.0 us would fall with it is not tested.

**The start** (498.3 for 475). Eight fills of k_rows, 0.91 each with 0.26 between them, are in the diff and not in my sum. The first split came 10.7 us behind its product (433.0 for 422.3), and 2.6 behind it in e17 (422.28; product ended at 419.64), which gave back 6.5 us of the start. The rest is landings, 3.0 each in my sum: the layout gave 13.6 (e9). With both mended the first transposed score is at 474.3 (e17), for 475.

**g = 1** (20.4 in the forecast, 28.9 in the trace, 23.9 with its transfers mended). A down with project_o takes 2.9 us and not 2.4: 1.8 of the 3.5. The transposes of the maxima wait for the split of q and k, 0.8. Low clock at the slot's head, where TensorE comes out of g = 0's wait, is 0.3 to 0.4 of the rest in e9 and e7; some 0.5 stays open. Of the 5 us beyond it 2 to 3 went with the layout, and among them is the cover that I had given the rank rows, "some 15 us": TensorE waited 1.6 us a batch for them. The other 2 to 3 are the pauses, which no term of my sum has.

**The stall of a normalise** (6.2 in the forecast) was sound as a mechanism, and too large. The reciprocal is 3.35 us, not 4.3. So the row from 16 to 32 elements, extended (3.4), was right, and the value between the two ends was not. The estimate of 4.3 from the Trainium skill ("VectorE: DVE Perf Modes", First, the fixed hardware budget) is 28% over the row. A block of 2.9 us was worth 4.7 in g = 2 and 3.2 in g = 0, which leaves 1.8 and 0.3 for the clock behind it; I took 2.0.

**g = 3 and g = 2 without the stall** (17.6 and 18.2): 17.5 in the changed kernel, 18.2 in e12. The chain through burst, hidden product, copy and exponential holds.

**The last batch and the end** (82 and 37; 96.5 and 41.6). Late sums are the smaller part of the last batch: g = 2 takes 25.1 us there for 23.6. g = 1 takes 31.2 for 19.0, and it holds the longest of the pauses, 6.3 us. In e8, where g = 1 is the same code and has no pause, it takes 22.2. By the same comparison the pauses and the low clock behind them made up 28 of the 161 us: 6 x 3.1 in the middle batches and 9.0 here. The end's chain was as told, and 5 us longer, with 12.7 us of wait ahead of the downs; e11 shows that 8.6 of such a wait, and 2.3 us of low clock behind it, are a matter of order.

**Batch 0** (75; 96.5, and 88.0 in e7, 69.9 in e17). It had three things that the sum lacked: late rows, late sums, and half clock in the loop of the maxima. I haven't parted them.

**The rivals.** "The sums come late" came true in its mechanism and its point (13.0 asked for, 23.8 there), and its time of 1265 was 94 us short, for it had 4.6 us a landing, nothing for the start and nothing for g = 1 and its pauses. "A short stall" was right on the reciprocal's size, which didn't matter while the sums were late. Of the signs that I had named as showing the forecast wrong, "VectorE's wait for ao_in" is the one that spoke: 79.6 us.

## What to carry to other kernels

Where a change sends a value through DRAM, write down for each slot the queue's issues in order with what each waits for. Add the landings in series, with a price from a copy of the same form under the same traffic, and compare with the moment at which the first in-order engine asks; a cover of 1 us is no cover. Put what an engine's queue will block on first, and loads that nobody waits for soon last, but follow each load that you put back to its reader's queue (e5). Before moving or cutting a long operation in a chain without slack, make it smaller: 32 columns in place of 512, at the price of two transfers that have a slot to land in, and with the moves that belong to it, took the ratio from 1.002 (e7) to 0.959 (e13). And before a run with one edit is said to have gained nothing, look in its trace for what else changed (e3).

## What the runs showed of the hardware that I had not expected

- A store of 192 KB as 3 parts of 32 rows took 6.6 us from its issue to that of the load behind it, and 2.1 us as 96 rows of one part.
- The reciprocal's time goes with the columns: 0.34 us for 128x32, 0.52 for 128x64, 3.35 for 128x512; a copy of 128x512 takes 0.43.
- In some runs ACT and VectorE stand together for 4 to 7 us late in the gathers of y_b in g = 1, with no releaser in the trace. In batch 4 of the changed kernel the transposed score starts at 945.37 and lasts 0.50; its exponential starts at 948.46. The runs with such pauses, and ACT's time in them, stand under the first table. The two waiting groups of the changed kernel:

```profile
ACT prob L783 <- remote: 20.9, 4, 6.3
DVE top L1395 <- remote: 20.4, 4, 6.0
```

What causes them is open. e1 to e4 ran on one chip and e16 on another, and the kernel before is slow on both (1240 and 1243 us, for 1218 to 1223 on the chips of the rest but e13). But e13 ran on the chip of e16 and has none, and the trace of the kernel before has 1.2 us in all of such standing at its exponentials. The comparison with e8 (see "The last batch and the end") puts their cost at 28 us in the changed kernel, 2% of its time. A ratio to the kernel before doesn't take that out, so ratios from different chips, or of runs with and without pauses (e14 with e16), are good to 1 or 2% only.
